# Attention by row tiles over streamed K and V, and an FFN with three banks for its first GEMM

## The reference

```python
# x: [16, 2048, 1024]; K, V: [4096, 1024]; w1: [4096, 1024]; w2: [1024, 4096]
scores = einsum('bld,sd->bls', x, K)
g = gelu(scores)
w = g / norm(g, axis=-1) * sqrt(4096)
x = layernorm(x + einsum('bls,sv->blv', w, V))

# act_quant: int8 by the row's maximum; weight_quant: -1, 0, 1 by the mean of |w|
h = act_quant(x) @ weight_quant(w1).T
h = depthwise_conv1d(h, conv_w, conv_b)      # three taps along the sequence
h = silu(h)
x = layernorm(x + act_quant(h) @ weight_quant(w2).T)
```

## Time and profile before

| | |
|---|---|
| three runs, median (lowest to highest) | 2286.78 us (2276.84 to 2377.11) |
| the profiled execution | 2274.48 us |
| its slowest core, span | 2272.9 us (the eight: 2256.0 to 2272.9) |
| granted clock of TensorE, all cores | 0.935 to 0.940 |
| busy: TensorE, VectorE, ScalarE, POOL | 1919.5, 1387.4, 1003.2, 546.7 us |
| read from HBM, written | 167.87 MB, 50.33 MB |

### The profile page before, as it was taken

How to read it: one execution, slowest core, us unless ns; L and a number is a source line. 1 busy time by engine, 2 the same in 40 slices (tenths; PEclk the granted TensorE clock), 3 DMA queues, 4 the chain that set the end, 5 groups by cost and what they waited for, 6 DMA issues and landing times.

```text
span 2272.9 us, 28317 instructions; the slowest of 8 cores (2256.0 to 2272.9 us)
## 1 busy us (share of the span) xinstructions
PE 1919.5 (84%) x8836; PEld 852.0 (37%) x8836; DVE 1387.4 (61%) x2087; ACT 1003.2 (44%) x1290; POOL 546.7 (24%) x523
## 2 busy tenths in 40 slices
PE   3659999988899899999367789888798888979888
PEld 1214444433444344444123334333343333434333
DVE  0335767575776745354257667677676767767673
ACT  1220605123050414242047575757657575665752
POOL 2000000000000000000036262544526264362630
PEclk9779999999999999999688899999999999999999
DMA  9993666466565521210520001111010111101111
GB/s 157 183 181 117 172 144 174 121 178 150 175 176 148 162 61 51 59 53 30 169 52 20 1 19 56 38 38 56 1 64 30 56 38 38 56 1 56 38 37 75
DMA packets 152886, 194.89 MB, mean 86 GB/s; under 512 B 53408, under 2 KB 98464, under 8 KB 152736
## 3 DMA queue, kind: packets, MB, share of 16 engines
q1 hardware_dynamic: 131872, 167.90, 25.0%
q0 software_dynamic: 20864, 25.17, 7.6%
HBM read 167.87 MB, written 50.33 MB: 96 GB/s over the span
## 4 chain that ended last, share of the span: by engine, by line
PE 50%; DVE 15%; DMA 10%; issue 10%; ACT 6%; POOL 6%; another core or an unknown queue 1%; SPq 1%; DVEq 1%; POOLq 0%; ACTq 0%
PE pA L390 19%; PE pA L760 14%; PE pB L353 9%; PE pB L602 6%; DMA wtmp<-w1T 5%; POOL R L673 5%; ACT ca L648 3%; DVE ca L668 2%; DVE htr L621 2%; DVE pm L695 1%; DMA R<-kT 1%; ACT R L690 1%; DVE acc L373 1%; DMA R<-w2T_sc 1%; DVE wqi L302 1%
## 5 line engine op out<-in xcount | busy, mean ns | idle before, releaser
L602 PE MATMUL pB<-yqTw,R 128*128 128x512 bf16 x2048 | 512.2, 397 | 129.7 <-DVE htr L621 109.2
L353 PE MATMUL pB<-xT_sb,R 128*128 128x512 bf16 x2048 | 476.7, 392 | 113.2 <-ACT R L361 77.6
L760 PE MATMUL pA<-R 128*128 128x512 fp8e4 x2048 | 489.2, 384 | 4.5 <-ACT R L749 4.5
L390 PE MATMUL pA<-R 128*128 128x512 bf16 x2048 | 459.8, 386 | 17.4 <-DMA R<-v 17.4
L673 POOL TENSOR_TENSOR R<-ca,R 128x512 f32<-128x512 f32 x256 | 337.3, 1319 | 482.8 <-DVE ca L668 377.7
L361 ACT ACTIVATE R<-pB 128x512 bf16<-128x512 f32 x256 | 151.2, 590 | 492.6 <-PE pB L353 492.1
L602 PEld LDWEIGHTS pB<-yqTw,R 128*128 128x128 fp8e4 x2048 | 198.8, 100 | 400.4 <-issue 195.5
L353 PEld LDWEIGHTS pB<-xT_sb,R 128*128 128x128 bf16 x2048 | 200.2, 100 | 380.3 <-issue 170.3
L390 PEld LDWEIGHTS pA<-R 128*128 128x128 bf16 x2048 | 202.4, 100 | 263.0 <-issue 33.9
L760 PEld LDWEIGHTS pA<-R 128*128 128x128 bf16 x2048 | 203.2, 99 | 260.4 <-issue 31.3
L648 ACT ACTIVATE ca<-htr,cwb_sb 128x512 f32<-128x512 f32 x256 | 207.0, 809 | 184.5 <-DVE htr L621 138.8
(11 more groups left out here) (84 smaller groups left out, 1019.3 us busy)
## 6 DMA issues: line engine op xcount, KB each, us to landing
wtmp<-w1T SPq DMA_DIRECT2D x128, 256.0 KB, 4.2
wtmp<-w2T SPq DMA_DIRECT2D x128, 256.0 KB, 3.5
z<-x SPq DMA_DIRECT2D x32, 512.0 KB, 4.1
y_sc<-z SPq DMA_DIRECT2D x32, 512.0 KB, 4.1
yw<-y_sc SPq DMA_DIRECT2D x32, 512.0 KB, 3.3
out<-yw SPq DMA_DIRECT2D x32, 512.0 KB, 2.6
xT_sb<-xT POOLq DMA_DIRECT2D x8, 1024.0 KB, 13.7
R<-kT POOLq DMA_DIRECT2D x8, 1024.0 KB, 62.2
```

What stands on the lines that cost most here:

```text
L353: O("tensor", lambda t, ss=ss, j=j, lo=lo: t.matmul(pB[:, lo:lo + TA], KT[:, j * S + 128 * ss:j * S + 128 * (ss + 1)], xT_sb[:, j * TA:(j ...
L390: O("tensor", lambda t, h=h, k=k, tt=tt, b0=b0: t.matmul(pA[:, 512 * (b0 + h):512 * (b0 + h) + dw], g_sb[:, k * TA + 128 * tt:k * TA + 128 ...
L602: O("tensor", lambda t, c=c, j=j, lo=lo: t.matmul(pB[:, lo:lo + TA], W1T[:, j * H + 128 * c:j * H + 128 * (c + 1)], yqTw[:, j * TA:(j + 1) ...
L760: O("tensor", lambda t, k=k, h=h, tt=tt, pr=pr: t.matmul(pA[:, 1024 * pr + 512 * h:1024 * pr + 512 * (h + 1)], hq[:, TA * k + 128 * tt:TA ...
```

## The change

**Attention.** K and V come in 16 parts each, and K, V and x lie in HBM so that a partition's part is one contiguous row. The weight loads wait for V's last part, and no weight step stands in block 0. In block 0 three row tiles are summed together, k outermost, in all four banks of `pA` and both of `pB`; tile 3 follows. The LayerNorm of a tile is now a list of eight steps (`ln1`); those of a block's last tile (in block 0, of tiles 1 to 3, without the multiply-adds of tiles 1 and 2) are put into `later` and stand one to a score group in the next block, ahead of the weight steps. In their place in the last row tile stand eight weight steps. The x loads, the y stores and the yqT stores move from SP to POOL.

**FFN.** `pC` becomes the third bank of `pB`; the row scales and the maxima use `pD` instead. `m3` goes round three banks, `ca` has three buffers, `add_taps` runs two chunks behind, `silu` and `part_max` one chunk later than before. The next window's row scales are made at chunks 9 and 10 into a second `S_sb`, with `pm` as the place of `diag`.

The diff, cut to what the text speaks of:

```diff
     UW = 512
+    nKc, nVc = 16, 16
+    kc_w = S // nKc
...
@@ -148,8 +150,8 @@
     O = sc.op
 
     pA = outer.enter_context(nc.psum_tensor("pA", [128, 2048], F32))
-    pB = outer.enter_context(nc.psum_tensor("pB", [128, 1024], F32))
-    pC = outer.enter_context(nc.psum_tensor("pC", [128, 512], F32))
+    pB = outer.enter_context(nc.psum_tensor("pB", [128, 1536], F32))
...
-            out=xT_sb[:].rearrange("p (j t) -> p j t", j=d8),
-            in_=xT_in.rearrange("(j p) t -> p j t", p=128)[:, :, TA * i:TA * (i + 1)]),
+            out=xT_sb[:], in_=xT_in[i]),
...
-            out=KT[:].rearrange("p (j s) -> p j s", j=d8)[:, :, kc_w * c:kc_w * (c + 1)],
-            in_=kT_in.rearrange("(j p) s -> p j s", p=128)[:, :, kc_w * c:kc_w * (c + 1)]),
+            out=KT[:, d8 * kc_w * c:d8 * kc_w * (c + 1)], in_=kT_in[c]),
...
-            out=V_sb[:].rearrange("p (c d) -> p c d", c=s32)[:, vc_n * c:vc_n * (c + 1), :],
-            in_=v_in.rearrange("(c p) d -> p c d", p=128)[:, vc_n * c:vc_n * (c + 1), :]),
+            out=V_sb[:, D * vc_n * c:D * vc_n * (c + 1)],
+            in_=v_in[:, D * vc_n * c:D * vc_n * (c + 1)]),
...
-        x_ld[n] = O("sync", lambda s, n=n, b=b: s.dma_start(
+        x_ld[n] = O("gpsimd", lambda s, n=n, b=b: s.dma_start(
...
-        yqTs_free[b] = O("sync", lambda s, n=n, b=b: s.dma_start(
+        yqTs_free[b] = O("gpsimd", lambda s, n=n, b=b: s.dma_start(
...
+    wst["free"] = [v_ok[-1]] * 3
...
+    def kcol(ss, j):
+        return d8 * kc_w * (128 * ss // kc_w) + kc_w * j + (128 * ss) % kc_w
...
+    later = []
+
+    def ln1(n, tt, zb, ps, banks, mm_ok, rl2_ok):
+
+        t = {}
+
+        def evac():
+            O("vector", lambda v: v.scalar_tensor_tensor(
+                z[zb][:], ps, rl2[:, tt:tt + 1], z[zb][:],
+                ALU.mult, ALU.add), W(mm_ok, rl2_ok, x_ld.pop(n)), "ve")
+            t["z"] = sc.cur("ve")
+            for free, k in banks:
+                free[k] = t["z"]
...
+            t["st"] = O("gpsimd", lambda s: s.dma_start(
+                out=y_sc[128 * n:128 * (n + 1), :], in_=z[zb][:]),
+                W(t["y"]), f"qy{zb}", 16)
...
+        def done():
+            quant1(1)
+            z_free[zb] = (t["st"], sc.cur("ve"))
+            if n + 3 < nA * nT:
+                load_x(n + 3)
+            pend_yq.append((n, sc.cur("ve")))
+
+        return [evac, stats, aggr, norm, maxabs, scales, lambda: quant1(0), done]
+
+    def row_norms():
...
+    def mm2(dst, tt, h, k, free):
+        O("tensor", lambda t: t.matmul(
+            dst, g_sb[:, k * TA + 128 * tt:k * TA + 128 * (tt + 1)],
+            V_sb[:, k * D + dw * h:k * D + dw * (h + 1)],
+            start=(k == 0), stop=(k == s32 - 1)),
+            W(g_ok[k], v_ok[k // vc_n], free if k == 0 else None),
+            "pe" if k == s32 - 1 else None)
...
-            wstep(1)
+            if later:
+                later.pop(0)()
+            elif i > 0:
...
+        while later:
+            later.pop(0)()
...
+        if i == 0:
+
+            places = [(pA[:, 0:512], pA[:, 512:1024]), (pA[:, 1024:1536], pA[:, 1536:2048]),
+                      (pB[:, 0:512], pB[:, 512:1024])]
+            pB_old = (pB_free[0], pB_free[1])
+            m_ok = {}
+            for k in range(s32):
+                for tt in range(3):
+                    for h in range(ndh):
+                        mm2(places[tt][h], tt, h, k, pB_old if tt == 2 else None)
+                    m_ok[tt] = sc.cur("pe")
+                if k == 3:
+                    rl2_ok = row_norms()
+            parts = [ln1(tt, tt, tt, ps, banks, m_ok[tt], rl2_ok) for tt, ps, banks in (
+                (0, pA[:, 0:D], ((pA_free, 0), (pA_free, 1))),
+                (1, pA[:, 1024:1024 + D], ((pA_free, 2), (pA_free, 3))),
+                (2, pB[:, 0:D], ((pB_free, 0), (pB_free, 1))))]
+            for p in parts:
+                p[0]()
+            for step in parts[0][1:]:
+                step()
+            later += parts[1][1:] + parts[2][1:]
+        for tt in range(3 if i == 0 else 0, nT):
...
+            steps = ln1(n, tt, zb, pA[:, 512 * b0:512 * b0 + D],
+                        ((pA_free, b0), (pA_free, b0 + 1)), mm_ok, rl2_ok)
+            if tt == nT - 1 and i + 1 < nA:
+                if i > 0:
+                    wstep(8)
+                later += steps
+                continue
+            for q, step in enumerate(steps):
+                step()
+                if i > 0 and q in (2, 7):
+                    wstep(2)
...
-    S_sb = sbuf("S_sb", [128, TA], F32)
-    diag = sbuf("diag", [128, TA], F32)
+    S_sb = [sbuf(f"S_sb{i}", [128, TA], F32) for i in range(2)]
     htr = [sbuf(f"htr{i}", [128, TA + 2], F32) for i in range(3)]
-    ca = [sbuf(f"ca{i}", [128, TA], F32) for i in range(2)]
+    ca = [sbuf(f"ca{i}", [128, TA], F32) for i in range(3)]
     ct = sbuf("ct", [128, TA], F32)
     runmax = sbuf("runmax", [128, TA], F32)
     pm = sbuf("pm", [128, TA], F32)
+    diag = pm
...
-        ok = rows_to_all(pC[:], fr["pC"], ready)
-        S_ok[w] = O("scalar", lambda s: s.activation(S_sb[:], pC[:], AF.Copy),
-                    W(ok, fr["S"]), "ac")
-        fr["pC"] = S_ok[w]
+        ok = rows_to_all(pDf[:], fr["pD"], ready)
+        S_ok[w] = O("scalar", lambda s: s.activation(S_sb[w % 2][:], pDf[:], AF.Copy),
+                    W(ok, fr[f"S{w % 2}"]), "ac")
+        fr["pD"] = S_ok[w]
...
-        lo = 512 * b
+        lo = 512 * (c % 3)
         for j in range(d8):
             O("tensor", lambda t, c=c, j=j, lo=lo: t.matmul(
                 pB[:, lo:lo + TA],
                 W1T[:, j * H + 128 * c:j * H + 128 * (c + 1)],
                 yqTw[:, j * TA:(j + 1) * TA], start=(j == 0), stop=(j == d8 - 1)),
-                W(yq_ok[w], w1_ok, ms_free[b]) if j == 0 else (),
+                W(yq_ok[w], w1_ok, ms_free[c % 3]) if j == 0 else (),
...
-        ms_free[b] = sc.cur("ve")
+        ms_free[c % 3] = sc.cur("ve")
...
-        prev = None
+        prev = []
...
-            taps_c = (c,) + taps(c)
-            if prev is not None:
-                add_taps(*prev)
-            prev = taps_c
-            if c >= 5 and c % 4 == 1:
-                silu(w1, c - 5, 4)
-            if c in (11, 19, 27):
-                part_max(c - 11, 8, 0, TA // 2, runmax if c == 11 else pm)
+            prev.append((c,) + taps(c))
+            if len(prev) == 3:
+                add_taps(*prev.pop(0))
+            if c >= 6 and c % 4 == 2:
+                silu(w1, c - 6, 4)
             if c in (12, 20, 28):
-                part_max(c - 12, 8, TA // 2, TA, runmax if c == 12 else pm)
-                if c > 12:
+                part_max(c - 12, 8, 0, TA // 2, runmax if c == 12 else pm)
+            if c in (13, 21, 29):
+                part_max(c - 13, 8, TA // 2, TA, runmax if c == 13 else pm)
+                if c > 13:
                     join_max()
             if c % 2 == 1 and halves:
                 quant(w, 1, halves.pop(0))
+            if c == 9 and w1 + 1 < nW:
+                s_ready = s_prep_a(w1 + 1)
+            if c == 10 and w1 + 1 < nW:
+                s_prep_b(w1 + 1, s_ready)
             if c >= 2:
                 step_due()
-        load_next = w1 + 1 < nW
 
         silu(w1, 28, 2)
-        add_taps(*prev)
+        add_taps(*prev.pop(0))
+        add_taps(*prev.pop(0))
         silu(w1, 30, 2)
-        if load_next:
+        if w1 + 1 < nW:
             load_window(w1 + 1)
-            s_ready = s_prep_a(w1 + 1)
         part_max(24, 4, 0, TA, pm)
         join_max()
         take(mm, 8)
-        if load_next:
-            s_prep_b(w1 + 1, s_ready)
...
```

182 lines of the change are left out of this document (87 added, 95 removed).

## The result

The changed kernel takes 2123.3 us (median of 4 runs, lowest 2119.9) against 2293.6 for the kernel before, measured beside it: ratio 0.928, 95% interval 0.9218 to 0.9343. It is faster, as forecast, but by less, and 8 us above the range. The profiled execution took 2122.96 us (span 2121.1) against 2274.48: 152 us less where the forecast had 226, that is 75 us over its sum.

| stage | before | forecast | after | off by |
|---|---|---|---|---|
| block 0 ends | 226.3 | 145 | 134.1 | -11 |
| blocks 1 to 7 | 870.2 | 848 | 869.4 | +21 |
| handover | 50.6 | 25 | 25.4 | 0 |
| FFN | 1125.8 | 1028 | 1092.2 | +64 |

The account below looks back on a forecast made before the run. TensorE bounds every stage, with 495 us of stalls. From 2,274.5: block 0 -81, blocks 1 to 7 -22, handover -25, six FFN windows -71, window 7's chunks -12, first window -15, giving 2,048 us; range 1,985 to 2,115.

Parts of the forecast that it names:

- TensorE and V at a tie: Block 0: three tiles' sums done at 122 us, V in at 120, so V nearly hidden; block 145 us, -81.
- The wait for x and a free bank: Block 0: x loads stand behind V in the same queue, 5 us; tile 3 needs its bank, so 127 us.
- the estimate was 94 for V: Block 0: the skill's 2.0 us plus bytes / 436e3 would put V in at about 94; forecast took 120.
- eight weight steps take 10 to 13 us, begun 3 us before the end: Blocks 1 to 7, last tile's end: leaves stalls of 1 us with sums, 5 with ternary steps; blocks -22 in all.
- 8 more, waits for loads included: Blocks with ternary steps: VectorE has about 57 to 60 us of work for a 55 us score phase, losing 8 more.
- Handover: Attention to FFN: both weight reloads issued about 55 us before block 7 ends; 25 instead of 50.6 us, -25.
- the tail: transposes wait 2 to 3 us, +1: FFN window's end: VectorE late at chunk 31, less the diagonal moved to chunk 9; tail +1, window about 122.5 us.
- the last 91.3 us are unchanged: End of the FFN, after window 7's chunks: no gain or loss counted.
- closing chain stays: FFN window 0: last chunk to first int8 tile unchanged; half the excess between chunks won, 110 us, -15.
- two chunks late: FFN: a third bank lets VectorE be two chunks late instead of one; a window's chunks 91 us instead of 103.2.
- The FFN rival: FFN: VectorE and ScalarE keep the windows since decoupling does little; windows of 129, total 2,100 us; chance 0.22.
- The slower side: Attention: POOL queue becomes the bound; at landings of 13.7 us, 2,135 us. Chance of slower 0.02, milder form 0.03.

Follow-up runs that it names:

- kv_old8: Changed kernel with K and V in the old layout and 8 parts each, block 0's order still changed: 2140.6 and 2148.2 us, ratio 0.9383.
- sp_queues: Changed kernel with x loads, y stores and yqT stores given back from POOL to the SP queue: 2161.7 to 2181.8 us, ratio 0.951.
- thin: Changed kernel with 1 weight step in place of 8 behind a block's last tile: 2135.0 us, ratio 0.935.
- best2: Changed kernel, FFN fed evenly, row scales' matmul at chunk 13, four load buffers, 3 weight steps behind last tile, none in last three score groups: 2034.4 and 2037.8 us.
- two_banks: Changed kernel with two banks instead of three for the FFN chunks, two-chunk distance kept: 2111.4 us.
- one_behind: Changed kernel with the FFN multiply-adds one chunk behind instead of two, three banks kept: 2175.5 us.
- even_mm4: Changed kernel with row scales' matmul at chunk 13 and second-GEMM steps given 3 in chunks 0 to 3, then 2 a chunk: 2050.9 to 2071.4 us, ratio 0.9014.
- spread: Changed kernel with the eight weight steps behind a block's last tile removed and put in its other tiles: 2127.2 us.
- buf4: Changed kernel with four buffers for the weight loads in place of three: 2105.1 to 2114.2 us, ratio 0.9238.
- skip_last: Changed kernel with no weight step in a block's last three score groups and 5 instead of 4 in each row tile: 2124.7 us, ratio 0.9282.
- best3: Against `best2`: weight steps earlier, six a row tile, 4 behind the last, and the weight scale's matmul one tile later: 1995.2 to 1998.5 us, ratio 0.8743.

## Why the prediction missed its range

Two steps failed, 85 us together, of which block 0 gave 11 back. In the FFN the forecast put TensorE's wait for the end of VectorE's chain at 2 to 3 us a window, and at nothing new in window 0 and at the end; it is 9 to 10 us a window, and 9 to 11 more than before in those two (+64 in that stage). In blocks 1 to 7 it had the eight weight steps done in 10 to 13 us from 3 us before the block's end, and a stall of 5 us where they are ternary; there it is 8 to 10 us, with a stall at the row norms besides (+21).

**Block 0 (-11 us).** Right in mechanism, TensorE and V at a tie; the sizes were too large in three places. V's last wait ends at 116.7 us for a forecast of 120, and the sums at 119.5 for 122. I took 6.2 us per MB as the nearest row, and it was 6.0 to 6.2. The wait for x and a free bank was 0.8 us where I had 5, for tile 0's multiply-add found its x landed when the last matmul of the tile ended (118.85). And tile 3 took 13.8 us, with no slow matmul, where I had 14 + 4. `kv_old8`, at the old rates, ended at 151.4. By the slope of the Trainium skill (DMA: Bandwidth & Descriptors, "Anatomy of one DMA — SWDGE (gpsimd) path") the estimate was 94 for V; the trace does not agree, with 116.7.

**Blocks 1 to 7 (+21).** The first three are 5 us over in all (350.8 for 346), with stalls of 4.4 and 2.9 us at the sixth group of blocks 2 and 3 instead of 1. The step that failed is "eight weight steps take 10 to 13 us, begun 3 us before the end". It nearly holds for sums (12 to 14 us, begun 2.4 to 2.6 before the end). Ternary steps took 15 to 17 us and began as the block ended, because a tile with four of them is already 14.0 us of VectorE against 13.9 of TensorE: behind block 4 so, with no stall before it. The forecast counted VectorE's work in the score phase (57 to 60 us in 55) and not in the tiles. The stall at the row norms, 7.9 and 7.0 us, it had only as "8 more, waits for loads included"; it overlooked that the kernel before has this stall too (4.27 and 5.09 us). Blocks 4 to 7 are 518.6 us, where I had 502. In the rows of blocks 5 and 6 the granted clock is 0.93 and 0.94, in blocks 1 and 3 it is 1.00.

**Handover (0).** Right, by its own steps; `sp_queues` shows that it is the queue, and `thin` and `best2` its condition, that the last weight step be stored more than 31 us before the end.

**FFN (+64).** The chunks are as forecast: 90 us in the windows for 91, 85.7 in window 7 for 91.5. The step that failed is "the tail: transposes wait 2 to 3 us, +1", and with it "the last 91.3 us are unchanged" and window 0's "closing chain stays". The transposes wait 9.0 us in windows 1 to 6, 10.0 at the end instead of 0.8, and 16.6 in window 0 instead of 6.0, 80.9 us in all, and matmuls run slowly behind. A window is 130.2 to 132.5 us where I had 122.5, which makes 50 for the six; the end is 11 over and window 0 is 9 over; window 7's chunks give 6 back. I had put down VectorE "two chunks late" as a gain and not asked who meets it at the end of the chain. The third bank, which I named first, gave nothing (`two_banks`); the distance of two chunks gave the gain in the chunks (`one_behind`). The FFN rival (VectorE and ScalarE keep the windows, 2,100) had nearly the right time of a window (129), for a wrong reason: `even_mm4` shows 122 with the same engines. That its total is nearer to the measured one than mine is luck.

**The slower side.** POOL's queue held nothing: `rstd` took 0.65 us, and the landings are the 5.1 and 3.8 us given above. The Trainium skill's rule on shared ports (SBUF — State Buffer, "SBUF: two separate sides"), which spoke against moving transfers to POOL, is not seen in the issues: the 32 x loads took 0.585 us each to issue with VectorE busy beside them. Whether VectorE held the shared port in those moments was not looked at.

**What stays open.** That small transfers of SP take some 10 us while x^T lands is shown; what holds them is not, for the two queues together keep the engines 72% busy in that stretch. Why the transposes still wait 4.4 us when fed evenly, and 16.6 in window 0, was not tried.

## What to carry to other kernels

A slack buffer moves a wait to the next place where the two engines must meet; look there (a reduction's result, a broadcast) before counting the gain, and first even out the order in which the fast engine feeds the slow one. When side work is moved, its end has a deadline (here the reload of the weights) and its share of a queue has a price, so move all of it in one plan: the four changes of one place each (`spread`, `thin`, `buf4`, `skip_last`) moved the time by -9 to +12 us, their combination by -56 (`best3` against `even_mm4`).

## What the runs showed of the hardware

- The cost of a MB written by the POOL queue with a change of type, all eight cores loading at once, depends on the row: 7.4 and 7.6 us at 1 KB, 6.2 and 6.3 at 2 KB, 6.0 to 6.2 at 4 KB.
- In the 12 us in which 1 MB of x^T is written by the POOL queue, 256 KB loads of the SP queue take 8.6 to 11.7 us to land (median of each of six blocks), though their median is 3.9 and 3.5 over the whole kernel; 64 KB stores take 8.2 to 9.8.
- Around a wait of 9 us the granted clock of a 41 us stretch is 0.87, and the 16 matmuls behind it take 5.46 us instead of 3.5.
